# Slot 20's two y additions as scaled copies on ScalarE, the last expert pair two slots later, and the last convolution taps one slot later

## What is computed

```python
x = x + layernorm(mamba(layernorm(x)))
x = x + layernorm(moe(layernorm(x)))
# mamba, per token t: u = silu(causal_conv4(x_in) + b), delta = softplus(dt @ W_dt + b_dt)
h = exp(delta * A) * h + (delta * u) * B_t      # 512 channels x 16 states
y = sum_n(h[:, n] * C_t[n]) + D_skip * u        # then y * silu(z) @ W_out
# moe: 2 shared gate/up/down blocks of 128 and 8 experts of 128, each token weighs its top 2
```

## Time and profile before

| | before |
|---|---|
| median of 3 runs | 2396.18 us (2395.93 to 2397.23) |
| profiled execution | 2396.12 us, its span 2394.3 us |
| busy: DVE, PE, POOL, ACT | 91%, 87%, 80%, 70% of the span |
| granted TensorE clock, mean | 0.932 of full speed |

### The profile page before, as it was taken

The page is one execution under the profiler, slowest core; times in us unless marked ns, Lnnn a source line. Parts: engine busy times, 40 slices in busy tenths (PEclk is TensorE's granted clock), DMA queues, the critical chain, the costliest instruction groups (busy, mean ns, idle before and its releaser), DMA issues. The chain is left out here.

```text
span 2394.3 us, 30302 instructions
## 1 busy us (share of the span) xinstructions
PE 2081.6 (87%) x9216; PEld 1359.5 (57%) x9216; DVE 2189.5 (91%) x3112; ACT 1666.7 (70%) x2484; POOL 1908.7 (80%) x1566
## 2 busy tenths in 40 slices
PE   6668989899898989989898998989889898996977
PEld 2345565656556565665656556565655656565544
DVE  2999999999999999999999999999999999998950
ACT  4557777777877776877777687777777777775632
POOL 3576897969889797888979788797988979698844
PEclk8759999999999999999999999999999999998989
DMA  4111121111121111211111121121111211111201
GB/s 130 37 36 44 61 61 49 59 57 58 53 62 60 52 56 56 61 54 59 58 54 49 54 71 58 54 58 52 56 54 63 62 50 58 49 57 47 68 21 45
DMA packets 92946, 134.27 MB, mean 56 GB/s; under 512 B 12000, under 2 KB 42976, under 8 KB 92784
## 3 DMA queue, kind: packets, MB, share of 16 engines
q1 hardware_dynamic: 92784, 132.34, 18.3%
HBM read 123.13 MB, written 9.18 MB: 55 GB/s over the span
## 5 line engine op out<-in xcount | busy, mean ns | idle before, releaser
L793 DVE TENSOR_TENSOR_SCAN h<-d_a,carry,d_bu 128x512 f32<-128x512 f32 x1024 | 1262.1, 1267 | 53.6 <-ACT d_a L615 45.4
L1024 POOL TENSOR_TENSOR d_bu<-delta_u,b_rows 128x1024 f32<-128x1024 f32 x512 | 1202.2, 2362 | 4.9 <-DMA b_rows<-b_rows_hbm 0.8
L615 ACT ACTIVATE d_a<-delta,a_neg 128x512 f32<-128x512 f32 x1024 | 696.4, 689 | 481.7 <-DVE h L793 479.9
L449 PE MATMUL ht<-ident,h 128*128 128x128 f32 x4096 | 624.0, 299 | 148.0 <-DVE y_t L803 141.1
L449 PEld LDWEIGHTS ht<-ident,h 128*128 128x128 f32 x4096 | 515.4, 153 | 371.2 <-DVE y_t L803 142.1
L803 DVE SCALAR_TENSOR_TENSOR y_t<-ht,c_t,y_t 128x512 f32<-128x512 f32 x896 | 621.2, 735 | 2.7 <-PE ht L449 2.0
L524 PE MATMUL ring<-x_t,w_gate_sb 128*128 128x512 f32 x640 | 321.0, 627 | 23.1 <-ACT delta L758 19.0
L531 PE MATMUL ring<-x_t,w_up_sb 128*128 128x512 f32 x640 | 301.9, 616 | 22.7 <-ACT silu_gate L708 22.5
L551 PE MATMUL dn<-w_down_sb,up_hidden 128*128 128x256 f32 x1280 | 304.3, 381 | 15.8 <-POOL up_hidden L1082 15.8
L1077 POOL TENSOR_TENSOR up_hidden<-silu_gate,up_hidden 128x512 f32<-128x512 f32 x160 | 204.6, 1278 | 125.9 <-ACT up_hidden L712 77.4
L551 PEld LDWEIGHTS dn<-w_down_sb,up_hidden 128*128 128x128 f32 x1280 | 235.9, 190 | 77.4 <-issue 28.7
(11 more groups left out here) (114 smaller groups left out, 1922.0 us busy)
## 6 DMA issues: line engine op xcount, KB each, us to landing
b_rows<-b_rows_hbm SPq DMA_DIRECT2D x256, 256.0 KB, 3.5
coef_rows<-coef_rows_hbm SPq DMA_DIRECT2D x128, 256.0 KB, 3.4
xa<-L_attn_x_in SPq DMA_DIRECT2D x16, 512.0 KB, 5.0
xr<-L_attn_x_in SPq DMA_DIRECT2D x16, 512.0 KB, 5.2
out<-xr SPq DMA_DIRECT2D x16, 512.0 KB, 2.9
w_in_sb<-L_attn_W_in_in SPq DMA_DIRECT2D x1, 1024.0 KB, 6.3
w_gate_sb<-L_ffn_experts_gate_in SPq DMA_DIRECT2D x2, 512.0 KB, 4.9
w_up_sb<-L_ffn_experts_up_in SPq DMA_DIRECT2D x2, 512.0 KB, 5.6
```

The costliest lines, as they stand in the source:

```text
L449: last = nc.tensor.transpose(HT[q % HTS][:, j * P:(j + 1) * P], H[:, (NS * c + n) % HS, j, a * P:(a + 1) * P], IDN[:, :])
L615: nc.scalar.activation(DA[i % DAS][:, :], DL[:, r, j, :], ACT.Exp, scale=ANEG[:, j, n:n + 1]).then_inc(ex.sem, 1)
L793: nc.vector.tensor_tensor_scan(H[:, (NS * s + n) % HS, j, :], DA[(n * J + j) % DAS][:, :], BU[:, (2 * n + j // 2) % 4, j % 2, :], CARRY[:, ...
L1024: nc.gpsimd.tensor_tensor(BU[:, (2 * n + h) % 4, :, :], DU[:, 2 * h:2 * h + 2, :], BB[:, n % 2, :].unsqueeze(1).to_broadcast([P, 2, T]), A ...
```

## The change

- The two additions of slot 20 (q = 14 and 15: n = 3, a = 2 and 3) are taken from DVE. ACT makes scaled copies of them (`side_state`, slot 20, behind the decay of that slot) into `YS`. That is the `xr` buffer of the same parity, whose result has been stored by then. PE adds them to the yd banks by transposing matmuls (`transpose_side`), four in slot 1 and four in slot 4. SP's reload of `xr` waits for the full yd banks.
- The last expert pair starts in slot 52 instead of 50 (the down matmuls of the pair before it move by two slots as well), and the y statistics move from slot 60 to 62.
- The DVE taps of j = 3 move from slot 11 to 12, behind scan 12, and so do the SiLUs of u for j = 2 and 3.
- POOL: the carry of the last state stands behind the inflow of slot 0 instead of before it, the y shift takes two operations instead of three (a subtraction), and the o shift two instead of one.

```diff
+        YS = XR[:, :, :, :].rearrange("p b a d -> p b (a d)").rearrange("p b (i d) -> p b i d", i=2)
-        scan, add_c, carry = stage("scan", NS * J), stage("add_c", (NS - 2) * NT), stage("carry_s", NS)
+        scan, add_c, carry = stage("scan", NS * J), stage("add_c", (NS - 2) * NT - 2), stage("carry_s", NS)
-        XIN_PE, TAP0_ACT, CONV = (3, 4, 7, 8), (4, 5, 8, 8), (6, 7, 10, 11)
+        XIN_PE, TAP0_ACT, CONV = (3, 4, 7, 8), (4, 5, 8, 8), (6, 7, 10, 12)
-        PAIR_AT = (12, 22, 32, 42, 50)
+        PAIR_AT = (12, 22, 32, 42, 52)
+        SIDE_SLOT = 20
-        Z_PE, Z_ACT, Y_STATS = 9, (8, 8, 9, 9), 60
+        Z_PE, Z_ACT, Y_STATS = 9, (8, 8, 9, 9), 62
-        SILU = {11: [("u", 2), ("u", 3)], 60: [("z", j) for j in range(J)]}
+        SILU = {12: [("u", 2), ("u", 3)], 60: [("z", j) for j in range(J)]}
+        SIDE_Q = ADDS[SIDE_SLOT]
@@ def added(c, q)
+            if q in SIDE_Q:
+                return y_side.sem, y_side.at(c, q - SIDE_Q[0] + 1)
@@ sync, slot 4
                         sp.wait_ge(out_st.sem, stored)
+                        sp.wait_ge(full["yd"].sem, full["yd"].at(s - 1))
                         sp.dma_start(XR[:, (s - 1) % 2, :, :], again)\
@@ tensor
+            def transpose_side(s, js):
+
+                pe.wait_ge(y_side.sem, y_side.at(s - 1))
+                for j in js:
+                    for i in range(2):
+                        a = SIDE_Q[i] % NT
+                        nc.tensor.matmul(yd_bank(j)[:, a * P:(a + 1) * P], YS[:, (s - 1) % 2, i, j * P:(j + 1) * P],
+                                         IDN[:, :], start=False, stop=False, is_transpose=True,
+                                         skip_group_check=True)
                         for j in (2 * half, 2 * half + 1):
                             transpose_y(s, lo, j)
+                        transpose_side(s, (2 * half, 2 * half + 1))
@@ scalar
+            def side_state(c, r, q):
+
+                n, a = q // NT, q % NT
+                act.wait_ge(ht_full.sem, ht_full.at(c, q + 1))
+                act.wait_ge(out_st.sem, out_st.at(c - 2))
+                nc.scalar.activation(YS[:, c % 2, q - SIDE_Q[0], :], HT[q % HTS][:, :], ACT.Copy,
+                                     scale=CT[:, r, a, n:n + 1]).then_inc(y_side.sem, 1)
@@ vector
-                dve.wait_ge(*added(c, q - NT))
+                dve.wait_ge(*added(c, q - NT if q - NT not in SIDE_Q else q - 2 * NT))
-                        if with_scan and q >= NT:
+                        if with_scan and q >= NT and q not in SIDE_Q:
                             add_state(s, r, q)
@@ gpsimd
-                    nc.gpsimd.tensor_tensor(MR["y"][:, :], MR["y"][:, :], MR["o"][:, :], ALU.add)\
+                    nc.gpsimd.tensor_tensor(MR["y"][:, :], MR["o"][:, :], MR["y"][:, :], ALU.subtract)\
-                    if t == 0 and ffn:
-                        keep_state(s - 1, o, NS - 1)
                     if with_scan and n + 1 < NS and t % 2 == 0:
                         inflow(s, n + 1, t % NT // 2)
+                    if t == 0 and ffn:
+                        keep_state(s - 1, o, NS - 1)
```

More of the change, by code:

```diff
@@ L155, in mamba_moe_kernel @@
         yd, y_first, y_last, xt = stage("yd", J), stage("y_first", NT), stage("y_last", NT), stage("xt", KM)
+        y_side = stage("y_side", 2)
         rstd = {w: stage(f"rstd_{w}_s", 2) for w in ("xa", "o", "x1", "y")}
@@ L162, in mamba_moe_kernel @@
         tap0 = stage("tap0", J)
-        shift = {w: stage(f"shift_{w}", n) for w, n in dict(xa=2, o=1, x1=2, y=3).items()}
+        shift = {w: stage(f"shift_{w}", n) for w, n in dict(xa=2, o=2, x1=2, y=2).items()}
         stream = stage("stream", 1)
-        scan, add_c, carry = stage("scan", NS * J), stage("add_c", (NS - 2) * NT), stage("carry_s", NS)
+        scan, add_c, carry = stage("scan", NS * J), stage("add_c", (NS - 2) * NT - 2), stage("carry_s", NS)
         stats = {w: stage(f"stats_{w}_s", 2 * NT) for w in ("xa", "o", "x1", "y")}
@@ L200, in mamba_moe_kernel @@
         DU_POOL = (58, 58, 60, 60)
-        Z_PE, Z_ACT, Y_STATS = 9, (8, 8, 9, 9), 60
+        Z_PE, Z_ACT, Y_STATS = 9, (8, 8, 9, 9), 62
         U_EARLY, HEAD_POOL = 7, 15
-        SILU = {11: [("u", 2), ("u", 3)], 60: [("z", j) for j in range(J)]}
-        SILU_FIRST = {11: SILU[11] + SILU[60]}
+        SILU = {12: [("u", 2), ("u", 3)], 60: [("z", j) for j in range(J)]}
+        SILU_FIRST = {12: SILU[12] + SILU[60]}
         ADDS = {t: (t - NT - 2, t - NT - 1) for t in range(NT + 2, SLOTS, 2)}
@@ L218, in added @@
                 return y_last.sem, y_last.at(c, q - SLOTS + NT + 1)
-            return add_c.sem, add_c.at(c, q - NT + 1)
+            if q in SIDE_Q:
+                return y_side.sem, y_side.at(c, q - SIDE_Q[0] + 1)
+            return add_c.sem, add_c.at(c, q - NT + 1 - (2 if q > SIDE_Q[1] else 0))
         def gate_slot(f):
@@ L671, in body @@
                         first_state(s, r, t - NT - 1)
+                    if with_scan and t == SIDE_SLOT:
+                        for q in SIDE_Q:
+                            side_state(s, r, q)
                     if ffn and t == 1:
@@ L999, in rstd_of @@
                   .then_inc(shift[w].sem, 1)
+                pool.wait_ge(shift[w].sem, shift[w].at(c, 1))
                 if w == "y":
-                    pool.wait_ge(shift["y"].sem, shift["y"].at(c, 1))
                     pool.wait_ge(shift["o"].sem, shift["o"].at(c))
-                    nc.gpsimd.tensor_tensor(MR["y"][:, :], MR["y"][:, :], MR["o"][:, :], ALU.add)\
+                    nc.gpsimd.tensor_tensor(MR["y"][:, :], MR["o"][:, :], MR["y"][:, :], ALU.subtract)\
                       .then_inc(shift["y"].sem, 1)
-                if w != "o":
-                    pool.wait_ge(shift[w].sem, shift[w].at(c, 2 if w == "y" else 1))
+                else:
                     nc.gpsimd.tensor_tensor(MR[w][:, :], MR[w][:, :], MINUS4[:, :], ALU.mult)\
```

## The result

| | before | after |
|---|---|---|
| median (8 runs each, side by side) | 2396.36 us | 2404.68 us |
| range | 2395.01 to 2397.49 | 2402.53 to 2407.1 |
| ratio, 95% interval | | 1.0036 [1.0025, 1.0047] |
| profiled execution, its span | 2396.12, 2394.3 | 2407.1, 2405.3 |

What follows compares the result with a forecast made beforehand. DVE, busy 91% of the span, was taken to bound the kernel. Per inner chunk +0.6 - 0.5 + 0.4 = +0.5, +7.5 for fourteen; chunk 15 and tail +0.7: 2396.1 + 8 = 2404 us, range 2377 to 2412.

Steps and rivals of the forecast that it cites:

- Part 1: Slot 20: its two additions leave DVE, 1.31 us less a chunk; a copy on ACT takes 0.68 us.
- Part 2: Behind slot 20: late copies and a lower PE clock make DVE wait about 2.0 us in slots 22 to 30.
- the second wait: Slot 20: PE's wait before the pair's transposes, after the coefficients; 0.61 us longer, so the clock falls in nearly every chunk.
- L: PE's chain from slot 20 to 30: time lost to the lower clock, 0 to 3.1 us, taken as 2.1.
- the prediction's formula: Slot 30: PE delivers 2.68 + 15.6 + L us after scan 20 starts; DVE wants the data at 18.55.
- Part 3: Slots 11 to 14: taps and SiLUs moved; scan 14 gains 0.91, scan 12 loses 0.42, net -0.49 us a chunk.
- Parts 4 and 5: Chunk's end and start: added y transposes, moved last pair and y statistics; together net +0.4 us a chunk (0 to +0.9).
- Part 4: Slots 1 and 4: eight more y transposes; the second four cost +0.44 us a chunk, +0.85 at half clock.
- (a): Slots 20 to 30: PE keeps its full clock, so Part 2 costs nothing; 2379 us (2376 to 2391), chance 0.25.
- (b): Behind slot 20: clock falls only for the shortest stretch, L 1.4 to 1.5; no difference, 2393 us, chance 0.22.
- (c): Slots 1 to 5: y transposes cost at the lower clock each time, +0.4 us a chunk; 2410 us, chance 0.03.
- (d): Slot 22: late copies make DVE wait; alone gives back 0.3 of 1.3 us; counted inside (a), no own chance.

Runs made afterwards that it cites:

- e3: The changed kernel with ACT's two copies of slot 20 put in front of that slot's decay instead of behind it: 2378.45 us, ratio 0.9923 to before.
- e4: The changed kernel without its first part: slot 20's additions stay on DVE, no copies and no transposes of them: 2390.31 us, ratio 0.9972 to before.
- e2: The kernel before, with four gate-sized matmuls on PE in front of slot 20's wait for the router's coefficients: 2396.47 us, ratio 0.9996.
- e1: The changed kernel with four gate-sized matmuls on PE in front of slot 20's wait for the router's coefficients: 2379.96 us, ratio 0.993 to before.
- f7: f5 with the taps of j = 3 and the SiLUs of u back in slot 11: 2387.11 us, ratio 0.996 to before.
- f5: e3 with six gate-sized matmuls on PE in slot 63: 2379.59 us, ratio 0.9928 to before.
- f3: e3 without the eight transposes of the copies a chunk, so two state terms of y are missing: 2369.97 us, ratio 0.9885 to before.
- f1: e3 with the last expert pair and the y statistics back in slots 50 and 60: 2379.53 us, ratio 0.9925 to before.
- f6: f5 with the last expert pair and the y statistics back in slots 50 and 60: 2429.62 us, ratio 1.0138 to before.
- f2: e3 with the taps of j = 3 and the SiLUs of u back in slot 11: 2380.76 us, ratio 0.9936 to before.

## Why the prediction was right, step by step

Forecast 2404, measured 2404.68. The path and its price came out as described: late copies, a late PE chain at the lower clock, and DVE waiting for it. One reason given on the way, why the clock falls, is not borne out as it stands. The sum hit so closely by some luck, since two terms were off by 0.15 us a chunk in opposite directions and the profiled execution, which the terms are read from, grew by 11.0 us and not by 8.3.

- **Part 1.** Slot 20 is shorter by 1.30 a chunk (predicted 1.31). A copy takes 0.672 us (0.68).
- **Part 2, the start.** PE's transposes start 2.75 us after scan 20 (2.68).
- **Part 2, the clock.** It falls behind slot 20 in every inner chunk, as forecast, of two kinds in turn: as in chunk 8, from 1.2 to 8.0 us after scan 20 starts, or as in chunk 9, from 2.35 to 5.76. The two kinds of chunk last 142.4 and 141.0 us. Chunk 9's stretches:

```profile
1374.00:1376.30 2.30, 1.04 (x8) 0.64 (x8) 2.20 (x6) 0.54 (x2) 2.30 (x2) 1.00 0.06 14
1376.30:1380.00 3.70, 2.47 (x9) 2.10 (x10) 3.35 (x4) 3.41 (x6) 1.68 (x1) 0.61 0.01 2
```

- **Part 2, the reason for the fall.** The prediction took it that the second wait, longer by 0.61 us, makes the clock fall in nearly every chunk. As the whole reason that is not borne out. In chunk 8 of after it fell at 1233.77, 0.06 us after the coefficients' transposes had ended (1233.71), when the second wait had hardly begun; only in chunks like 9 did it fall 1.2 us or more into that wait, or just behind it. In e3 there is no second wait, and it falls in all of chunks 1 to 14. In e4 the waits are 2.00 and 0.97 us in each of chunks 3 to 13, and it falls in seven of these eleven. What after has in every chunk and the kernel before only in two of three is the first wait of 2.00 us or more. So the fall in every chunk was forecast rightly, for a reason that is at most a part of it; that is luck as far as it goes.
- **Part 2, the price.** Slots 22 to 30 are 1.75 a chunk longer than before (predicted 2.0 less 0.1), slots 20 to 30 together 0.43 (0.6). Without waits slots 20 to 30 take 19.84 us (e3). So DVE loses 2.0 us here, as predicted: 2.5 to 2.7 in chunks like 8 and 1.4 to 1.6 in chunks like 9. What was too small is the credit for what the kernel before lost: not 0.07 but 0.24 a chunk (21.40 against 21.16 in e2), because chunk 10's slots 20 to 30 take 21.83 where the others take 21.16. The 0.21 printed in the earlier trace rows is only a part of that. L, read as half of PE's work at the lower clock, is 2.6 to 2.8 us in chunks like 8 and 1.5 to 1.7 in chunks like 9, 2.1 on average, as taken. (With L = 2.1 the prediction's formula gives a wait of 1.8, not the 2.0 that it wrote; so its 15.6 is short by some 0.15.) The formula also fits two more kernels. e1 has the start of after and L = 0: 2.76 + 15.6 = 18.4 against the 18.55 at which DVE wants the data, no wait. e3 starts at 1.04, so it can bear L = 1.9; its clock is low for 3.4 us, all of it work, 1.7 lost, no wait.
- **Part 3.** Slots 11 to 13 -0.49 (predicted -0.49), with 0.34 of idle before scan 12 (0.4). f7 against f5 shows it alone: 0.50. In chunk 0 slots 11 to 13 lost 1.1 (9.60 for 8.51), as said.
- **Parts 4 and 5.** +1.00 in slots 0 to 5 and -0.46 in slots 54 to 63, net +0.54 for +0.4. The term mis-sized is that of the y transposes: 0.57 by f3's median, 0.61 by after against e4, for 0.44 and then 0.2 given back. The 0.44 is right where the clock does not interfere: slots 0 to 5 take 12.24 us in chunks like 9 of after, where it is back 3 us after the chunk's start, and 11.80 in most chunks of e4. In chunks like 8 it stays low until 5.4 us, and they take 12.8. So the clock at the chunk's start cost more, where the prediction gave something back for it. The pair's move is worth zero by f1: what slot 60 gains (0.46) POOL takes in slot 1. POOL's inflow is late at scan 2 (1.15), which the prediction left open between scans 2 and 4, but called 0.4 there.
- **Part 4, the lower clock each time.** The added transposes of slot 4, by line and operation (ns: shortest, median, longest):

```profile
L479 PE MATMUL dn<-ident,xr x64: 272/273/273, 195.0 to 2312.2; 128*128 128x128 f32 x64
```

  All 64 took the same time, at a granted clock of 1.00. Of the 64 in slot 1 18 took longer, up to 421 ns, and all 18 began at a granted clock of 0.50; the median is 273. The Trainium skill, in "TensorE: Matmul & The Clock Gate", Part 4, says that the full clock does not engage for transposes; the measurement disagrees.
- **Sum.** From the start of chunk 1 to that of chunk 15 the profiled execution grew by 8.7 us (forecast 7.5), chunk 15 by 0.9 and the tail by 1.2 (0.7 together), chunk 0 by 0.3 (about 0): 11.0 in all, where the forecast's terms make 8.

The rivals: (a), 2379, did not come about in after, but both e1 and e3 reach it (2380 and 2378). Its condition, that the clock stays full, is sufficient (e1) and not necessary: an earlier start does it as well (e3). What the prediction could have said and did not is that the 0.69 of the decay ahead of the copies was a matter of order, not of need. (b) would have needed L of 1.5, which only the chunks of chunk 9's kind come near, with 1.5 to 1.7. (c) is ruled out by the durations. (d), the copies alone late, is ruled out by e1, where the copies are just as late and nothing waits.

What stays open: what decides whether the clock falls behind slot 20, and why its pattern settles into two kinds of chunk in turn in after, three before, and nearly one in e3. No run here settles it.

The kernel to keep is e3_copies_first: 0.8% faster than before [0.6%, 0.9%] and 1.1% faster than after, by moving three lines.

## What to carry to other kernels

Work moved to an idle engine must not be put behind an instruction there that waits for something it does not need: putting the copies ahead of it lets e3's chain start 1.7 us earlier, and that decided between +8 and -18 us. Where PE's chain sets when DVE gets its data, add up the chain once at full clock and once at half, and compare both with the time at which DVE wants it. The clock can cost as much as the gap ahead of the chain, or more: in after 1.65 us of gap were followed by 1.5 to 2.8 lost to the clock. Matmuls into a bank that is overwritten anyway can hold the clock up. They pay only where they stand ahead of the gap in PE's order and end before the chain can start (e1: 3.6 us of them, and the chain starts no later); f5's ended too late, f6's stood behind the gap, and in the tail, where PE sets the end, they cost their own length.

## What was not expected of the hardware

- A 128x512 fp32 matmul is two PE instructions: four in the source gave eight in the trace, 3.6 us at the full clock, and six gave twelve, 5.32 us at 1.00 and 5.96 where the first part ran at 0.50.
- In chunk 8 of after PE was busy for 13.66 of the 15 us before slot 20, at a granted clock of 1.00. Then, after 2.00 us of idle time and 1.04 of work, it fell to 0.50. It fell behind slot 20 in every chunk of e3 as well. With 3.60 us of matmuls in place of the first gap and 0.29 of idle behind the coefficients it stayed at 1.00 there in chunks 1 to 14 of e1. But in chunks 7 to 9 of f2, with 2.00 to 2.22 us of idle time in the same place, it did not fall: the gap at the place itself does not decide it alone.
- The state of the clock at one place carries over to another: in f2 the taps in slot 11 changed how the clock stood at the chunk's start, and 0.29 of the 0.46 us a chunk that they cost came back there.
